# Edge stage of a hybrid conv/attention kernel: the indirect gathers of a chunk gated by the column count of an earlier chunk

## Chip, cores, metric

The kernel runs on one core of one Trainium2 chip. The metric is the device time of one execution in microseconds (us).

## What is computed

The kernel runs a whole network of six layers on 8 images of 32 x 32 x 128 (retention, 3x3 convolution, windowed sum, mixture of 16 experts, windowed attention, and a last mixture of 4 experts whose gates come from a graph attention layer). The change touches only the graph attention. Cut to that:

```
h = (x_flat @ W_gat).reshape(M, 4, 4)                  # M = 8192 nodes, 4 heads of 4
src, dst = edge_index plus one self loop per node      # 524288 edges
e = leaky_relu(a_src[src] + a_dst[dst], 0.2)
ee = exp(e - max over the edges of the same dst)
denom = segment_sum(ee, dst)
agg = segment_sum(h[src] * ee / denom[dst], dst)       # then layernorm, top-2 gates
out = sum over 4 experts of gate * (gelu(x @ W1 + b1) @ W2 + b2)
```

## The kernel before

Edges are sorted and reduced before this stage, so that each of the 128 partitions holds columns of edge keys. A *column* is 128 edges, one a partition; a *chunk* is 16 columns (CHUNK); a *turn* is two chunks (AHEAD = 2), which use buffer halves s = 0 and 1. In the profiled execution TensorE does 320 columns, so 20 chunks, numbered 0 to 19, in ten turns. The first eight turns are a plain loop and the others stand behind a check of the number of edges left.

Each engine has its own program, and they meet by semaphores.

- GpSimd, `fetch(c, s)` (L941 to L948): waits until VectorE has written the indices of chunk c (`records_used`), does a marker instruction (`take_wait`, L813), and then issues 32 indirect DMAs: for each column one gather of 128 source records of 20 floats from `src_dram` and one of 128 target records of 4 floats from `dst_dram` (L947). Each increments `gathered[s]` by 16 when landed. There are 21 fetches, for chunks 0 to 20.
- VectorE, `edge_turn` (L2600 on): for each column t of chunk c the product `rh[:, t % 4]` (L2597, 128 x 1280 floats, from `spread_columns`, L2594 on) of a one-hot matrix and the weighted values, in a ring of RH = 4 buffers. After column 12 (FFN_AT) of chunk c it prepares chunk c+1 (`prepare`, L2565 on: two one-hot matrices) and calls `attend` for it (L2574 on), which waits for all 32 gathers of chunk c+1 to land. Then it does columns 12 to 15, waits for ScalarE's exponential (L1882), weighs the values, and writes the indices of chunk c+3 (`index`, L2558 on, in the half that chunk c+1 has just finished with), which releases GpSimd. So the fetch of a chunk c can begin when VectorE is at the end of chunk c-3, and must have landed by column 12 of chunk c-1.
- TensorE, `edge_column` (L1481 on): waits for the product of a column, adds it into three PSUM banks with three matmuls (six records in the profile), and increments `scattered` (L1489). For the first six turns (chunks 0 to 11) each column is followed by a quarter of an expert step of the last layer (`expert_part`, L1463 on, L1472 and L1478: two records).
- ScalarE, `experts` (L1884 on): the gelu (L1890) and the bias (L1895) of these expert steps, and the exponential of a chunk (L1882). SP stores each expert result in DRAM (L776).

`scattered` is the counter that the change touches. It starts with one increment of RH = 4 from TensorE (L1459) and grows by one for each finished column. VectorE waits for it before each column, so that buffer t % 4 is free:

```
dve.wait_ge(scattered, c * CHUNK + (t + 1))
```

`since(eng, signal, value)` is a wait that leaves itself out where the value is a constant of zero or less. The window stage before the edge stage also has runs of indirect DMAs, 16 gathers of 512-byte rows each (`gather_made`, L917), beside VectorE, ScalarE and TensorE work of the attention layer.

## Time and profile before

| | us |
|---|---|
| median of 3 runs | 4359.78 |
| lowest and highest | 4357.78, 4380.45 |
| profiled execution, device time | 4385.87 |
| its span | 4384.0 |
| TensorE busy (share of the span) | 3178.3 (72%) |
| VectorE busy | 2720.1 (62%) |
| ScalarE busy | 1739.6 (40%) |
| GpSimd busy | 1541.9 (35%) |

PE is TensorE's matmuls, PEld its weight loads, DVE VectorE, ACT ScalarE, POOL GpSimd and SP SyncE. Times are counted from the start of the span. The number in brackets after an instruction of a timeline is the engine's idle time just before it, with what ended it; "remote" there means that the profile names no instruction of this core as the one that ended the wait, and "issue" that it shows nothing that was waited for. A row with a count merges several instructions that follow each other.

### The profile page before, as it was taken

What the parts mean: (1) busy time and instruction counts of PE and PEld (TensorE: products, weight loads), DVE (VectorE), ACT (ScalarE), POOL (GpSimd) and SP (SyncE); (2) the same over time, 40 slices, a digit from 0 to 9 for tenths busy, and PEclk for the clock granted to TensorE, in tenths of its full rate; (3) what the DMA queues carried; (4) which work ended last, traced back from release to release, by engine and by line L of the source; (5) the groups of instructions that cost most, each with busy time, mean ns of one, the idle gap of its engine ahead of it and who ended that gap; (6) DMA issues with size and microseconds to landing.
All of it is one profiled execution on the core that took longest, in us unless ns stands there. A gap on an engine that the chain in (4) does not pass through costs nothing.

```text
span 4384.0 us, 50073 instructions
## 1 busy us (share of the span) xinstructions
PE 3178.3 (72%) x13837; PEld 1510.7 (34%) x13839; DVE 2720.1 (62%) x3836; ACT 1739.6 (40%) x3383; POOL 1541.9 (35%) x1297
## 2 busy tenths in 40 slices
PE   1799999999956637763477888658786787766648
PEld 0222222222212216651355666224343333433322
DVE  2678787787837769997755666215344343554467
ACT  0587787777845625542333454321111111000000
POOL 0211111111003459997333220343443534444500
PEclk9999999999976759996677777679898888877878
DMA  6544234442311127762011010111010100000014
GB/s 214 140 130 121 48 116 120 128 109 55 94 59 62 68 75 239 215 206 82 20 33 29 26 36 12 45 39 27 18 22 22 22 19 18 11 3 3 4 48 182
DMA packets 247387, 319.87 MB, mean 73 GB/s; under 512 B 52301, under 2 KB 183437, under 8 KB 246681
## 3 DMA queue, kind: packets, MB, share of 16 engines
q1 hardware_dynamic: 217496, 296.77, 22.2%
q0 software_dynamic: 29696, 20.97, 2.9%
q8 instruction: 67, 1.10, 0.1%
q14 instruction: 128, 1.04, 0.1%
HBM read 170.95 MB, written 146.67 MB: 72 GB/s over the span
## 4 chain that ended last, share of the span: by engine, by line
PE 23%; another core or an unknown queue 15%; DVE 7%; issue 5%; ACT 1%; DMA 1%; DVEq 0%; SPq 0%; ACTq 0%
PE banks L1487 10%; PE banks L1307 2%; PE banks L1478 2%; PE banks L1472 2%; PE banks L1367 1%; DVE arena L2408 1%; PE banks L1375 1%; PE banks L1350 1%; DVE keys L2363 1%; DMA keys<-experts_dram 1%; PE banks L1551 1%; PE banks L1399 0%; DVE mx L2420 0%; ACT arena L1815 0%
## 5 line engine op out<-in xcount | busy, mean ns | idle before, releaser
L1487 PE MATMUL banks<-arena 128*128 128x512 f32 (+1 forms) x1920 | 804.4, 567 | 192.6 <-DVE arena L2597 126.0
L2597 DVE TENSOR_TENSOR arena<-arena,banks 128x1280 f32<-128x1280 f32 x320 | 466.3, 1485 | 673.0 <-remote 454.6
L1487 PEld LDWEIGHTS banks<-arena 128*128 128x128 f32 x1920 | 393.4, 207 | 663.3 <-issue 511.9
L2127 DVE TENSOR_TENSOR arena<-banks,arena 128x512 f32<-128x512 f32 x512 | 317.7, 683 | 108.6 <-PE banks L1000 82.6
L813 POOL TENSOR_TENSOR pool_spare<-pool_spare 128x1 f32<-128x1 f32 x54 | 16.7, 309 | 1001.3 <-DVE edges_now L2562 703.4
L947 POOL DMA_INDIRECT arena<-src_dram,edges_now x336 | 318.1, 947 | 105.9 <-issue 105.9
L2127 DVE TENSOR_TENSOR keys<-banks,arena 128x512 f32<-128x512 f32 x512 | 317.7, 683 | 60.6 <-PE banks L1000 37.8
L947 POOL DMA_INDIRECT arena<-dst_dram,edges_now x336 | 317.8, 946 | 102.5 <-issue 102.5
L904 POOL TENSOR_TENSOR arena<-arena 128x256 f32<-128x256 f32 x144 | 339.4, 2391 | 17.4 <-ACT arena L1787 17.2
L2363 DVE TENSOR_TENSOR keys<-keys 128x2048 f32<-128x2048 f32 x132 | 339.6, 2612 | 1.9
L1666 ACT ACTIVATE arena<-arena 128x512 f32<-128x512 f32 x512 | 287.0, 619 | 130.6 <-DVE arena L2127 89.1
L1000 PE MATMUL banks<-arena 96*128 96x512 bf16 x1024 | 281.6, 389 | 41.6 <-DVE arena L2127 31.6
L1666 ACT ACTIVATE keys<-keys 128x512 f32<-128x512 f32 x512 | 281.1, 617 | 55.3 <-PE banks L1023 46.7
L1478 PE MATMUL banks<-arena 128*128 128x512 f32 x256 | 154.7, 697 | 183.7 <-ACT arena L1890 177.0
L1895 ACT ACTIVATE keys<-banks,mb 128x512 f32<-128x512 f32 x64 | 44.0, 687 | 528.5 <-remote 304.2
L1844 ACT ACTIVATE arena<-arena,mx 128x128 f32<-128x128 f32 x256 | 99.6, 391 | 332.7 <-DVE mx L2421 318.0
L835 POOL TENSOR_TENSOR work<-work,keys 128x512 f32<-128x512 f32 x32 | 41.0, 1280 | 504.3 <-ACT keys L1602 504.3
L1307 PE MATMUL banks<-arena 128*128 128x64 bf16 x1152 | 151.2, 306 | 86.3 <-DVE arena L2408 74.8
L1000 PEld LDWEIGHTS banks<-arena 96*128 96x128 bf16 x1024 | 80.6, 98 | 346.8 <-DVE arena L2127 122.9
L1890 ACT ACTIVATE arena<-banks,mb 128x512 f32<-128x512 f32 x128 | 86.6, 687 | 266.8 <-remote 112.5
L825 POOL TENSOR_TENSOR keys<-keys 128x512 f32<-128x512 f32 x32 | 40.7, 1271 | 399.9 <-DVE keys L2034 399.9
L1307 PEld LDWEIGHTS banks<-arena 128*128 128x128 bf16 x1152 | 142.7, 148 | 109.6 <-DVE arena L2408 85.1
(399 smaller groups left out, 5804.8 us busy)
## 6 DMA issues: line engine op xcount, KB each, us to landing
sorted_dram<-zeros SPq DMA_DIRECT2D x8, 8192.0 KB, 29.1
arena<-in_w SPq DMA_DIRECT2D x150, 384.0 KB, 4.0
arena<-parts_dram SPq DMA_DIRECT2D x192, 128.0 KB, 4.8
experts_dram<-keys SPq DMA_DIRECT2D x64, 256.0 KB
keys<-experts_dram SPq DMA_DIRECT2D x8, 2048.0 KB, 8.6
parts_dram<-nodes SPq DMA_DIRECT2D x16, 768.0 KB, 3.3
slot_out_dram<-arena SPq DMA_DIRECT2D x40, 256.0 KB, 4.4
arena<-sorted_dram SPq DMA_DIRECT2D x150, 64.0 KB, 3.3
```

Of the source, the lines that this page charges most:

```text
L904: pool.tensor_tensor(slot_hid[:, j % RING], slot_silu[:, j % RING], slot_up[:, j % RING], ALU.mult)\
L947: pool.indirect_dma_start(to[:, s, t, :], None, table[:, :], bass.IndirectOffsetOnAxis(edges_now[:, s, n, t:t + 1].bitcast(U32), 0)).then_ ...
L1000: pe.matmul(banks[:, j, :], k_st[0:STACK, head, a * P:(a + 1) * P], q_st[0:STACK, head, halves(qh)], start=True, stop=True).then_inc(score ...
L1307: last = pe.matmul(out, count_low[:, r, :, t], count_high[:, r, :, t], start=start and t == 0, stop=stop and t == CHUNK - 1, skip_group_ch ...
L1472: pe.matmul(banks[:, 4 + c, :], m1[:, e, c * P:(c + 1) * P], xn_pair[s][:, halves(h)], start=True, stop=True).then_inc(m_h, 1)
L1478: pe.matmul(banks[:, 6 + i % 2, :], m2[:, e, c, :], mh[:, 2 * (i % 2) + c, :], start=(c == 0), stop=(c == CHUNKS - 1)).then_inc(m_out, 1)
L1487: last = pe.matmul(banks[:, bank, 0:part.shape[1]], ohl[:, s, t, :], part, start=False, stop=False, skip_group_check=True)
L1666: act.activation(a_slots[r % 2][:, j, :], p_slots[r % 2][:, j, :], ACT.Abs).then_inc(absolute, 1)
L1844: act.activation(sc[:, k % 2, j, :], sc[:, k % 2, j, :], ACT.Exp, bias=mx[:, k % 2, 1, j:j + 1], accum_out=mx[:, k % 2, 2, j:j + 1]).then_ ...
L2127: dve.tensor_tensor(p_slots[r % 2][:, j, :], banks[:, j, :], table[:, PER_GROUP * g + j, at:at + HALF], ALU.mult).then_inc(masked, 1)
L2363: dve.tensor_tensor(vo[:, t], vi[:, 0], vi[:, 1], ALU.max if t else ALU.min).then_inc(sort_step, 1)
L2597: dve.tensor_tensor(rh[:, t % RH], oha[:, s, t:t + 1, :].broadcast_to([P, VALS, NB]), vals[:, t, :].unsqueeze(2).broadcast_to([P, VALS, NB ...
```

## The change

GpSimd gets, before the gathers of each even column t, a wait for `scattered` and a no-operation that carries it. The value is 16 c + t - 12. So that it is positive for the chunks at the start, `scattered` begins at RH + CHUNK = 20 in place of RH = 4, and VectorE's waits for it are raised by CHUNK = 16. With the start value of 20, a value of 16 c + t - 12 is reached when 16 (c - 2) + t columns are finished by TensorE, that is, t columns of chunk c-2. Four gathers (two columns of sources and targets) stand between two such waits.

```diff
@@ fetch (GpSimd) @@
                 for t in range(CHUNK):
+                    if t % 2 == 0:
+                        since(pool, scattered, c * CHUNK + (RH - CHUNK + t))
+                        pool.nop(nofuse=True)
                     for n, (to, table) in enumerate(((srcrec, src_dram), (dstrec, dst_dram))):
@@ TensorE, the clearing matmuls @@
-            last.then_inc(scattered, RH)
+            last.then_inc(scattered, RH + CHUNK)
@@ spread_columns (VectorE) @@
-                    dve.wait_ge(scattered, c * CHUNK + (t + 1))
+                    dve.wait_ge(scattered, c * CHUNK + (CHUNK + t + 1))
@@ VectorE, before the first prepare @@
-            dve.wait_ge(scattered, RH)
+            dve.wait_ge(scattered, RH + CHUNK)
```

## Rows read from the trace of the kernel before

**Rows 1.** The page: busy tenths of POOL in 40 equal slices of the span.

```profile
POOL 0211111111003459997333220343443534444500
```

**Rows 2.** Waits, 2911 to 4203 us: who for whom, total us, times, longest.

```profile
POOL pool_spare L813 <- DVE edges_now L2562: 501.8, 19, 32.9
DVE arena L2597 <- remote: 454.6, 48, 18.9
...
ACT keys L1895 <- remote: 286.0, 12, 28.8
```

**Rows 3.** Timeline of GpSimd, one fetch: start us, duration us, instruction.

```profile
3262.24 0.96 POOL L947 DMA_INDIRECT arena<-src_dram,edges_now  x1 [0.49 <-issue]
...
3301.02 0.94 POOL L947 DMA_INDIRECT arena<-dst_dram,edges_now  x1 [0.30 <-issue]
```

**Rows 4.** Timeline of TensorE in the same chunk.

```profile
3260.66 2.31 PE L1487 MATMUL banks<-arena 128*128 128x512 f32 x6
...
3284.72 2.31 PE L1487 MATMUL banks<-arena 128*128 128x512 f32 x6
3286.86 1.02 PE L1472 MATMUL banks<-work,arena 128*128 128x512 f32 x2
...
3308.69 2.08 PE L1478 MATMUL banks<-arena 128*128 128x512 f32 x2 [13.74 <-ACT arena L1890]
```

**Rows 5.** Timelines of VectorE and ScalarE in the same chunk.

```profile
3276.47 1.49 DVE L2597 TENSOR_TENSOR arena<-arena,banks 128x1280 f32<-128x1280 f32 x1 [2.94 <-PE banks L1487]
3289.83 1.49 DVE L2597 TENSOR_TENSOR arena<-arena,banks 128x1280 f32<-128x1280 f32 x1 [11.88 <-remote]
3306.65 5.68 DVE L2597 TENSOR_TENSOR arena<-arena,banks 128x1280 f32<-128x1280 f32 x4 [15.34 <-remote]
...
3307.37 0.69 ACT L1895 ACTIVATE keys<-banks,mb 128x512 f32<-128x512 f32 x1 [27.39 <-remote]
```

**Rows 6.** Timelines of TensorE and ScalarE, the last two chunks.

```profile
4162.31 45.07 PE L1487 MATMUL banks<-arena 128*128 128x512 f32 x120 [2.48 <-DVE arena L2597]
...
4160.89 0.26 ACT L1882 ACTIVATE arena<-arena 128x64 f32<-128x64 f32 x1 [59.63 <-DVE arena L2582]
4197.10 0.26 ACT L1882 ACTIVATE arena<-arena 128x64 f32<-128x64 f32 x1 [35.95 <-DVE arena L2582]
```

**Rows 7.** Timeline of GpSimd: the markers of the fetches in chunks 0, 12, 18.

```profile
2911.39 0.19 POOL L813 TENSOR_TENSOR pool_spare<-pool_spare 128x1 f32<-128x1 f32 x1 [32.48 <-DVE edges_now L2562]
...
3744.35 0.20 POOL L813 TENSOR_TENSOR pool_spare<-pool_spare 128x1 f32<-128x1 f32 x1 [28.05 <-DVE edges_now L2562]
...
4108.10 0.19 POOL L813 TENSOR_TENSOR pool_spare<-pool_spare 128x1 f32<-128x1 f32 x1 [19.46 <-DVE edges_now L2562]
```

**Rows 8.** Timelines of GpSimd and VectorE: a run of 16 gathers.

```profile
2191.32 1.19 POOL L917 DMA_INDIRECT arena<-slot_out_dram,arena  x1 [0.18 <-issue]
...
2210.65 0.94 POOL L917 DMA_INDIRECT arena<-slot_out_dram,arena  x1 [0.30 <-issue]
...
2214.17 1.89 DVE L2456 SCALAR_TENSOR_TENSOR work<-banks,bout,work 128x512 f32<-128x512 f32 x3 [14.37 <-remote]
```

**Rows 9.** Timeline and waits (2560 to 2592 us): a looser run of 16.

```profile
2560.45 1.02 POOL L917 DMA_INDIRECT arena<-slot_out_dram,arena  x1 [0.45 <-issue]
2566.14 0.95 POOL L917 DMA_INDIRECT arena<-slot_out_dram,arena  x1 [4.67 <-issue]
...
2585.84 1.34 POOL L917 DMA_INDIRECT arena<-slot_out_dram,arena  x1 [0.30 <-issue]
...
DVE work L2456 <- PE banks L1394: 4.3, 1, 4.3
```

**Rows 10.** Timelines of GpSimd and ScalarE: the end of 64 gathers in one run.

```profile
2877.96 0.95 POOL L947 DMA_INDIRECT arena<-dst_dram,edges_now  x1 [0.30 <-issue]
...
2886.09 0.69 ACT L1890 ACTIVATE arena<-banks,mb 128x512 f32<-128x512 f32 x1 [4.21 <-remote]
```

**Rows 11.** Windows: busy us of each engine, TensorE's granted clock, DMA share, GB/s.

```profile
2911.00:3745.00 834.00, 640.32 (x1536) 309.16 (x1537) 352.19 (x363) 135.53 (x188) 365.90 (x397) 0.87 0.10 22
```

## Prediction

> **What bounds the kernel now.** The page's slices come first [rows 1]: POOL's tenths show the gathers that the change edits, from slice 26 on (some 2800 us), with POOL never over half busy. That stretch is the edge stage. The waits of 2911 to 4203 us come next [rows 2]. Three numbers matter. VectorE's column product (L2597) waits 454.6 us in 48 pieces for something the profile can't name ("remote"), ScalarE's L1895 waits 286.0 us in the same way, and GpSimd waits 501.8 us for the next chunk's indices, so it is idle a good third of the stage.
>
> The timeline of one chunk tells what the nameless waits are. GpSimd issues the chunk's 32 gathers from 3262.24 to 3301.96, (3301.02 - 3262.24) / 31 = 1.25 us apart [rows 3]. TensorE keeps a pace of (3284.72 - 3260.66) / 8 = 3.01 us a column (six matmul records of 2.31 us in all, and an expert part of two) until 3287.9, and then stands 13.74 us before the next expert part [rows 4]. VectorE's products at 3289.83 and 3306.65 come 11.88 and 15.34 us after the last, and ScalarE's L1895 comes after 27.39 us of idling [rows 5]. VectorE froze at 3276.47 + 1.49 = 3277.96, 15.7 us into the gathers, when 12 or 13 were out. ScalarE and VectorE both run freely again at 3306.65 to 3307.37, some 5.4 us after the last gather ended. So a dense run of gathers freezes two engines that have nothing to do with it, and TensorE starves.
>
> One chunk is the control. Chunk 19 has no gathers beside it: TensorE does 20 columns in 45.07 us without a gap, 2.25 us each, and ScalarE's exponentials are 35.95 us apart, where the chunk before took 59.63 [rows 6]. A chunk's gathers thus cost 24 us there. With the experts beside it, 12 chunks (0 to 11) take (3744.35 - 2911.39) / 12 = 69.4 us [rows 7], against 16 x 3.01 = 48.2 us of unbroken TensorE: 21.2 us of freezing each. Chunks 12 to 17 take (4108.10 - 3744.35) / 6 = 60.6 us [rows 7].
>
> **Why spacing can help.** The freeze must depend on density for the change to be worth anything. The window stage has runs of 16 gathers. The run from 2191.32 to 2210.65 is 1.29 us apart and froze VectorE for 14.4 us, until 2214.17, 2.6 us after its last gather [rows 8]. The run from 2560.45 to 2585.84 is 1.69 us apart (one pause of 4.67 us after its first gather), and the longest wait of VectorE's L2456 in it is 4.3 us, for a named TensorE matmul, with no nameless wait in the whole view [rows 9]. The thaw comes 2.6 us after 16 gathers and 5.4 us after 32, so each gather leaves (5.4 - 2.6) / 16 = 0.18 us of undone work: something serves a gather in 1.25 + 0.18 = 1.43 us. After 64 in one run ScalarE's last late operation starts at 2886.09, 7.2 us after the end at 2878.91, which says less per gather, (7.2 - 5.4) / 32 = 0.06 [rows 10]. My service time is 1.43 us, an estimate, the upper of the two, as it comes from runs of the length at issue.
>
> **The change part by part.** *The counter* starts at 20 in place of 4 and VectorE waits for 16 more: the same wait on the same column, one immediate, cost nothing.
>
> *The gate.* Per chunk GpSimd gets 8 waits with a no-operation to carry each, 7 with effect inside a chunk and the first at its border. The gate of columns t and t+1 opens when TensorE (it is TensorE's count, so a column that is multiplied) has finished t columns of the chunk two places ahead. Its own price does not show in the trace; the bounds are nothing (it fits in the 0.30 us between two gathers) and the 0.49 us between GpSimd's marker and its first gather [rows 3], so 0 to 4 us a chunk. I take 0.15 each, 1.2 us a chunk, nearer to the plain gap because only one instruction and a register sum are added. While GpSimd waits anyway it is hidden; in the chunks without experts it is not, but there it spaces.
>
> *What queues behind it.* Behind a closed gate stand the rest of the chunk's gathers and the next chunk's fetch, and only VectorE's attend waits for them, at its twelfth column of the next chunk. The last gate opens at 14 of 16 columns, so the last four gathers end about 6 us into the next chunk. VectorE, up to four columns ahead of TensorE, asks for them 8 x 3.01 = 24 us into it, so some 18 us are spare. SP's queue is not passed; its expert stores share the DMA engines with the gathers and meet them thinner.
>
> *Chunks with experts (0 to 11).* Two columns take 6.02 us and four gathers 5.0 us, so the gate holds and gathers come every 6.02 / 4 = 1.50 us, over 1.43: no backlog and no freeze, 48.2 us a chunk. The margin is 5%, so I put 49.5 us. 12 x (69.4 - 49.5) = 239 us saved. Who is late next is TensorE alone: VectorE's 16 products of 1.49 us [rows 5] and its preparation fit in 48 us.
>
> *Chunks without experts (12 to 18).* Two columns take 4.5 us, less than four gathers, so the gate is open whenever TensorE is at pace and does not space anything. The run freezes VectorE after about 16 us as before, TensorE uses up its four columns (9 us) and stops, the gate shuts, GpSimd pauses, and the backlog of some 3 us drains. Such a cycle is 16 + 9 + 3 = 28 us for about 20 gathers, 1.4 us each, or 45 us a chunk; TensorE restarts at half clock (2.08 us for the two-matmul part that takes 1.02 [rows 4]), which adds about 5. I take 50 us: 7 x (60.6 - 50) = 74 us saved. The bounds are GpSimd's own 32 x 1.25 + 3 = 43 us and today's 60.6.
>
> *Sum.* 239 + 74 = 313 us. The profiled execution took 4385.87 us (span 4384.0), so it would take 4073. The median of the three runs is 4359.78, 26.1 lower; against it the forecast is 4359.8 - 313 = 4047 us.
>
> **The rivals.**
> 1. *Only the chunks with experts gain* (the change does not do what it says in the rest, where the gate never shuts). For it: the 4.5 against 5.0 us. Against it: a frozen TensorE does shut the gate. 4359.8 - 239 = 4121 us. Chance 0.15.
> 2. *The freeze comes later but comes.* If a gather's service is nearer 1.69 than 1.43, the margin of 5% is none, and only half of the freezing goes: 4359.8 - 313 / 2 = 4203 us. For it: no row of the trace lies between 1.29 and 1.69. Chance 0.13.
> 3. *The freezes are not the gathers'* but belong to fetching the loop's code or to something periodic; then 4360 us. Against it: the last chunk runs the same code without one [rows 6]. Chance 0.04. The Trainium skill speaks for this one twice. "Runtime: NRT & Kernel Launch", section "Instruction fetch mechanics", says that a taken branch out of the loaded window stalls until the page is fetched; by that rule the stalls would stay, and the trace disagrees in the last chunk. "Trainium Architecture — The Big Picture", section "What this means for kernel authors", says that SBUF's engine side and DMA side can't contend and that only the port pair of VectorE and GpSimd is a lock; by that rule gathers could not hold up ScalarE and the sum would be 0 us, and ScalarE's 27.39 us disagree [rows 5].
> 4. *Slower: rest is what resets the freeze, not density.* Today the first 12 gathers of a chunk are free after 20 to 30 us of idle GpSimd. If a pause under 1 us gives back none of that, all 32 pay. A paying gather costs 21.2 / 20 = 1.06 us with experts and 24 / 20 = 1.2 without, so 12 x 12 x 1.06 + 7 x 12 x 1.2 = 253 us more: 4613 us. It decides from the second chunk on, where the rest has gone. Against it: the looser run of 16 went by with no nameless wait [rows 9], although it also had fewer than 32. Chance 0.06.
>
> **How the numbers follow.** The forecast has 0.62, and its own range is 3975 (48.2 and 43 us a chunk: 12 x 21.2 + 7 x 17.6 = 378 us saved, 3982, less a few us) to 4100. The full range reaches up through rivals 1 and 2, to 4205, and leaves out rivals 3 and 4 and the tails, about 0.15. Half a per cent, 22 us, is about what a measurement of this kernel can tell from no change. Faster by more: 0.62 + 0.15 + 0.13 = 0.90. Within: 0.04. Slower by more: 0.06.
>
> **What would show it.** In the changed profile, gathers of chunks 2 to 13 come in fours every 6.0 us with a pause of about a microsecond; the nameless waits of L2597 and L1895 are near 0 before chunk 12; GpSimd's markers are 48 to 50 us apart there and 43 to 52 us after; TensorE's granted clock in that stretch rises from 0.87 [rows 11] to near 1. The forecast is wrong if nameless waits of over 5 us go on inside the expert chunks (rival 2), if chunks 12 to 18 stay at 60 us (rival 1), or if freezes fill whole chunks (rival 4).

## The result, and the profile after

The changed kernel takes 4012.34 us (median of 4 runs, 4007.11 to 4034.18) where the kernel before, on the same chip, takes 4370.11 us (4 runs, 4357.78 to 4386.33). The ratio is 0.9189, 95% interval 0.9138 to 0.9239. The forecast was 4047 us, in a range of 3975 to 4205, so the direction and the range hold and the gain was somewhat larger than the sum.

The profiled execution took 4014.97 us, with a span of 4013.1 us, 370.9 us less than the one before. First the page of the changed kernel: engine totals, the slices of GpSimd and of TensorE's granted clock, and the groups of the edge stage (busy, mean ns | idle before, and what ended it). Line numbers are three higher than before: L950 is the gather, L2600 the column product, L1490 its matmuls, L1893 the experts' gelu and L1898 their bias.

```profile
PE 3101.9 (77%) x13837; PEld 1493.8 (37%) x13839; DVE 2725.1 (68%) x3836; ACT 1743.6 (43%) x3383; POOL 1545.4 (39%) x1297
POOL 0211111111110256799873222202466666666500
PEclk9999999999996675899856777677799999999968
L1490 PE MATMUL banks<-arena 128*128 128x512 f32 (+1 forms) x1920 | 742.9, 533 | 57.5 <-DVE arena L2600 53.0
L2600 DVE TENSOR_TENSOR arena<-arena,banks 128x1280 f32<-128x1280 f32 x320 | 468.8, 1486 | 318.2 <-PE banks L1490 222.4
L950 POOL DMA_INDIRECT arena<-src_dram,edges_now x336 | 318.4, 948 | 241.0 <-PE banks L1490 115.7
```

GpSimd's tenths in the edge stage now stand at 6 in eight slices running, where they changed between 3 and 5 [rows 1]. The gathers are as long and as many as before; what changed is that their engine waits for TensorE (the last line), and VectorE's wait is for TensorE too.

The waits of the changed kernel, from 2900 to 3830 us (sum, times, longest), answer to [rows 2]:

```profile
DVE arena L2600 <- PE banks L1490: 222.4, 146, 8.5
DVE arena L2600 <- remote: 44.7, 11, 8.3
POOL arena L950 <- PE banks L1490: 116.9, 69, 12.3
POOL arena L950 <- remote: 30.9, 8, 4.7
ACT arena L1893 <- remote: 4.3, 2, 2.2
```

VectorE's nameless waits fell from 454.6 to 44.7 us. ScalarE's were 286.0 us in the bias [rows 2] and 90.0 in the gelu (L1890, in the same view); now the bias has none and the gelu (L1893) 4.3. Nearly all of what is left lies in the chunks without experts: 43.8 of VectorE's 44.7 us are from 3481 to 3835, and all 30.9 of GpSimd's. These last are new. GpSimd too now has waits that the profile can't name.

GpSimd in an expert chunk (start, busy, line, [idle before]) comes in fours, as [rows 3] did not:

```profile
3454.77 0.94 POOL L950 DMA_INDIRECT arena<-src_dram,edges_now  x1 [1.32 <-PE banks L1490]
3456.01 0.95 POOL L950 DMA_INDIRECT arena<-dst_dram,edges_now  x1 [0.30 <-issue]
...
3458.51 0.95 POOL L950 DMA_INDIRECT arena<-dst_dram,edges_now  x1 [0.30 <-issue]
3460.78 0.95 POOL L950 DMA_INDIRECT arena<-src_dram,edges_now  x1 [1.32 <-PE banks L1490]
```

From one four to the next are 3460.78 - 3454.77 = 6.01 us, 1.50 a gather.

ScalarE's exponentials mark the chunks best, as there is one at the same point of each. Those of chunks 0, 12 and 20 (the last is the one past chunk 19) in the kernel before, and then in the changed one:

```profile
2909.82 0.26 ACT L1882 ACTIVATE arena<-arena 128x64 f32<-128x64 f32 x1
3742.67 0.26 ACT L1882 ACTIVATE arena<-arena 128x64 f32<-128x64 f32 x1
...
4197.10 0.26 ACT L1882 ACTIVATE arena<-arena 128x64 f32<-128x64 f32 x1 [35.95 <-DVE arena L2582]
```

```profile
2888.20 0.26 ACT L1885 ACTIVATE arena<-arena 128x64 f32<-128x64 f32 x1
3468.91 0.26 ACT L1885 ACTIVATE arena<-arena 128x64 f32<-128x64 f32 x1
...
3825.04 0.26 ACT L1885 ACTIVATE arena<-arena 128x64 f32<-128x64 f32 x1 [37.02 <-DVE arena L2585]
```

The stretch with experts (12 chunks, called A below) went from 832.9 to 580.7 us, 69.4 to 48.4 a chunk, and saves 252. The stretch behind it (B, eight intervals, the last without gathers beside it) went from 454.4 to 356.1 and saves 98. Together 350 of the 370.9 us. Of the rest, 21.6 lie ahead of chunk 0's exponential (2909.82 against 2888.20) and do not belong to the change: GpSimd's marker that opens the stage stood between 2764 and 2802 us in thirteen of the fourteen kernels traced here (2753 in the other), and what comes ahead of it is work that no edit touches.

The windows of the changed kernel over the two stretches (length, then PE, PEld, DVE, ACT and POOL busy, the granted clock, DMA share, GB/s), to be held against [rows 11]:

```profile
2889.80:3481.00 591.20, 590.38 (x1563) 297.37 (x1564) 362.45 (x364) 140.32 (x190) 367.86 (x399) 1.00 0.14 31
3481.00:3850.00 369.00, 296.78 (x763) 149.93 (x761) 228.44 (x236) 2.06 (x8) 211.86 (x229) 0.92 0.08 4
```

With experts TensorE is busy for 590.38 of 591.20 us, and granted 1.00 (its higher level, 2.4 GHz) where it had 0.87. That stretch has next to nothing left but TensorE's own work.

### The profile page after: what moved, and what is told of

It is laid out like the page before. It is cut to its first block and busy times, and to the rows that moved or that the text cites. A ratio compares the mean times of both kernels' runs of the same rounds, so it can differ in the third digit from the quotient of the medians.

```text
span 4013.1 us, 50374 instructions
## 1 busy us (share of the span) xinstructions
PE 3101.9 (77%) x13837; PEld 1493.8 (37%) x13839; DVE 2725.1 (68%) x3836; ACT 1743.6 (43%) x3383; POOL 1545.4 (39%) x1297
## 5 line engine op out<-in xcount | busy, mean ns | idle before, releaser
L1490 PE MATMUL banks<-arena 128*128 128x512 f32 (+1 forms) x1920 | 742.9, 533 | 57.5 <-DVE arena L2600 53.0
L2600 DVE TENSOR_TENSOR arena<-arena,banks 128x1280 f32<-128x1280 f32 x320 | 468.8, 1486 | 318.2 <-PE banks L1490 222.4
L1490 PEld LDWEIGHTS banks<-arena 128*128 128x128 f32 x1920 | 370.3, 194 | 481.0 <-issue 414.1
L950 POOL DMA_INDIRECT arena<-src_dram,edges_now x336 | 318.4, 948 | 241.0 <-PE banks L1490 115.7
L950 POOL DMA_INDIRECT arena<-dst_dram,edges_now x336 | 318.0, 947 | 109.9 <-issue 108.7
L2130 DVE TENSOR_TENSOR keys<-banks,arena 128x512 f32<-128x512 f32 x512 | 317.8, 684 | 60.8 <-PE banks L1003 38.3
L1003 PE MATMUL banks<-arena 96*128 96x512 bf16 x1024 | 282.6, 390 | 40.4 <-DVE arena L2130 30.9
L1893 ACT ACTIVATE arena<-banks,mb 128x512 f32<-128x512 f32 x128 | 87.9, 688 | 237.2 <-PE banks L1475 128.0
L1481 PE MATMUL banks<-arena 128*128 128x512 f32 x256 | 138.4, 631 | 53.1 <-ACT arena L1893 40.5
L917 POOL DMA_INDIRECT arena<-slot_out_dram,arena x128 | 159.8, 1249 | 43.1 <-issue 42.9
```

The lines of the kernel that those rows point to most:

```text
L917: pool.indirect_dma_start(made[:, j, :], None, slot_out_dram[:, :], bass.IndirectOffsetOnAxis(rows_now[:, j:j + 1].bitcast(U32), 0)).then_ ...
L950: pool.indirect_dma_start(to[:, s, t, :], None, table[:, :], bass.IndirectOffsetOnAxis(edges_now[:, s, n, t:t + 1].bitcast(U32), 0)).then_ ...
L1003: pe.matmul(banks[:, j, :], k_st[0:STACK, head, a * P:(a + 1) * P], q_st[0:STACK, head, halves(qh)], start=True, stop=True).then_inc(score ...
L1481: pe.matmul(banks[:, 6 + i % 2, :], m2[:, e, c, :], mh[:, 2 * (i % 2) + c, :], start=(c == 0), stop=(c == CHUNKS - 1)).then_inc(m_out, 1)
L1490: last = pe.matmul(banks[:, bank, 0:part.shape[1]], ohl[:, s, t, :], part, start=False, stop=False, skip_group_check=True)
L2130: dve.tensor_tensor(p_slots[r % 2][:, j, :], banks[:, j, :], table[:, PER_GROUP * g + j, at:at + HALF], ALU.mult).then_inc(masked, 1)
```

## The experiments

Each kernel is either the kernel before or the changed one with the edit shown. "Lead" is the time from GpSimd's first marker of the stage to chunk 0's exponential, A and B are the stretches above. "Thaw" is the time from the first gather of a run to the start of the operation that ends the last long nameless wait in it (ScalarE's, in the chunks with experts). The table gathers the results (a dash: not read), and each kernel is taken up below. Times are those of the profiled executions for the two kernels of the case, else medians or single runs; lead, A and B are read in each kernel's one profiled execution. The kernels ran on different chips, and the kernel before had medians of 4354 to 4378 us beside them.

| kernel | us | lead | A (a chunk) | B |
|---|---|---|---|---|
| before (profiled execution) | 4385.87 | 111.5 | 832.9 (69.4) | 454.4 |
| changed (profiled execution) | 4014.97 | 110.8 | 580.7 (48.4) | 356.1 |
| instruction between, no wait | 4313.97 | - | 822.2 (68.5) | 445.1 |
| gate for expert chunks alone | 4107.62 | 113.0 | 579.0 (48.3) | 450.8 |
| gate every 8 columns | 4118.99 | 110.7 | 652.1 (54.3) | 390.6 |
| gate every column | 4019.22 | 115.9 | 579.0 (48.3) | 351.5 |
| paced to 1.335 us, no gate | 4260.82 | 99.6 | 764.0 (63.7) | 417.3 |
| paced to 1.389 us | 4126.09 | 94.1 | 682.1 (56.8) | 379.9 |
| paced to 1.446 us | 3958.68 | 49.9 | 580.7 (48.4) | 354.2 |
| paced by a longer fill | 4014.41 | 52.6 | 602.7 (50.2) | 400.3 |
| small source records | 4352.70 | - | 827.0 (68.9) | 450.5 |
| half of the records | 4379.28 | - | 842.5 (70.2) | 458.1 |
| changed, once more | 4012.55 | 110.7 | 580.6 (48.4) | 352.6 |
| gate, and a paced lead | 3989.10 | 49.7 | 607.9 (50.7) | 356.8 |

### Is it the wait, or any instruction between the gathers?

On the kernel before:

```diff
                 for t in range(CHUNK):
+                    if t % 2 == 0:
+                        pool.nop(nofuse=True)
```

> The kernel before with the eight no-operations of a fetch and no wait in front of them. Backlog theory (each gather leaves 0.18 us undone at a distance of 1.25 us, and the freeze starts when some 2 us have piled up): the gathers stay at 1.25 to 1.3 us, chunks with experts stay at 68 to 70 us and the others at 60 to 61, time within 1% of before, 4330 to 4400 us. Rival (any break in the stream of gathers, even an instruction between them, is enough): near the changed kernel, 4010 to 4100 us.

Measured 4313.97 us in one run (4378.02 before on the same chip). The 64 us look like a gain, but the edge stage began some 46 us earlier, while A and B together are only 20 us shorter, and each chunk still freezes at the same point: the thaw comes 44.9 to 45.1 us after the first gather (44.6 in the first fetch behind the lead). The no-operation alone does next to nothing. It is the wait that counts.

### Which chunks does the gate help?

On the changed kernel, the gate is left off in the fetches of chunks 14 on:

```diff
-            def fetch(c, s):
+            def fetch(c, s, gated=True):
...
-                    if t % 2 == 0:
+                    if gated and t % 2 == 0:
...
-            with pool.Fori(0, IMAGES) as turn:
+            with pool.Fori(0, IMAGES - LEAD) as turn:
...
+            for turn in range(IMAGES - LEAD, IMAGES):
+                fetch(turn * AHEAD + 1, 1, turn == IMAGES - LEAD)
+                fetch(turn * AHEAD + 2, 0, False)
...
-                            fetch(turn * AHEAD + 1, 1)
-                            fetch(turn * AHEAD + 2, 0)
+                            fetch(turn * AHEAD + 1, 1, False)
+                            fetch(turn * AHEAD + 2, 0, False)
```

> The changed kernel with the gate only in the fetches of chunks 1 to 13, that is, beside the chunks with experts; the fetches of chunks 14 to 20 are ungated. If the gate works in both stretches as the changed profile reads (252 us from chunks 0 to 11, 98 us from 12 to 19), this takes the changed time plus 98 us, about 4110 us, with ungated chunks of 60 us. Rival (the chunks without experts gained only because the stage came into them with less backlog): under 4040 us.

4107.62 us: A stays at 579.0 and B goes back to 450.8, that of the kernel before. So in B too it is the wait in front of the gathers that saves the 98 us, although a column there (2.25 us) is quicker than its two gathers. The timeline of the changed kernel shows how. GpSimd, in the fetch of chunk 15:

```profile
3525.78 0.96 POOL L950 DMA_INDIRECT arena<-src_dram,edges_now  x1 [2.62 <-PE banks L1490]
...
3549.59 0.95 POOL L950 DMA_INDIRECT arena<-dst_dram,edges_now  x1 [0.30 <-issue]
3554.81 0.95 POOL L950 DMA_INDIRECT arena<-src_dram,edges_now  x1 [4.27 <-remote]
```

VectorE beside it:

```profile
3552.61 5.74 DVE L2600 TENSOR_TENSOR arena<-arena,banks 128x1280 f32<-128x1280 f32 x4 [6.64 <-remote]
```

And TensorE:

```profile
3519.46 28.09 PE L1490 MATMUL banks<-arena 128*128 128x512 f32 x78
3554.15 24.70 PE L1490 MATMUL banks<-arena 128*128 128x512 f32 x60 [6.61 <-DVE arena L2600]
```

Twenty gathers run without a pause from 3525.78 on. VectorE then stands 6.64 us before its product at 3552.61, TensorE runs dry and stands 6.61 us, and GpSimd stands 4.27 us before the 21st gather. The cycle is 3554.81 - 3525.78 = 29.03 us for 20 gathers, 1.45 each. GpSimd's markers in this stretch are (3756.31 - 3522.95) / 5 = 46.7 us apart.

It looks as if a dry TensorE had shut the gate, but it had not. The trace has all 1920 matmul records of the 320 columns, six each, so the columns can be counted. This gate asks for ten columns of chunk 13. The 78 records in the first row above are the last column of chunk 12 and twelve of chunk 13, and the tenth of these was finished at 3543.25, 7.3 us before GpSimd came to the gate at 3550.54. The same count for all eleven pauses of over 1 us that GpSimd makes at a gate from the fetch of chunk 15 on finds the columns finished 1.2 to 9.0 us before it came (and likewise finished before it came for 14 and 11 pauses in two kernels below, the changed one once more and the one with a gate every column). In this stretch GpSimd is not held back by an unfinished column. It is caught by the freeze itself, in the wait that the change gave it, and so ends its dense run after some 20 gathers in place of 32. What is late is taken up below. Whether a wait for a column long finished would do as well was not tried.

### How dense may the gathers be in a burst?

On the changed kernel, one gate for eight columns, and in another kernel one for every column:

```diff
-                    if t % 2 == 0:
+                    if t % 8 == 0:
```

> The changed kernel with a gate at every eighth column in place of every second: the same mean rate beside the experts, but in runs of 16 gathers. Backlog theory: it peaks at 16 x 0.18 = 2.9 us, so nameless waits of 3 to 8 us show in ScalarE and VectorE at the end of each run, partly hidden by the four columns in hand; chunks with experts 48 to 54 us, time 4010 to 4100 us. Rival (only the mean rate counts): no nameless waits, 48.1 us a chunk, equal to the changed kernel within 0.5%.

4118.99 us and 54.3 us a chunk in A, a little over the upper end of what was expected. Runs of 16 gathers freeze a little each time. GpSimd's first and last gather of one such run:

```profile
3058.62 0.95 POOL L950 DMA_INDIRECT arena<-src_dram,edges_now  x1 [9.64 <-PE banks L1490]
...
3077.35 0.94 POOL L950 DMA_INDIRECT arena<-dst_dram,edges_now  x1 [0.30 <-issue]
```

and ScalarE at its end:

```profile
3081.21 0.69 ACT L1893 ACTIVATE arena<-banks,mb 128x512 f32<-128x512 f32 x1 [1.51 <-remote]
```

The last nameless wait ends 3081.21 - 3058.62 = 22.59 us after the first gather, 1.41 us for each of 16, although GpSimd had put the last of them behind it at 3078.29. In the kernel before, 32 gathers from 3262.24 thaw at 3307.37 [rows 3, 5]: 45.13 us, 1.41 for each again. That was the first sign that the thaw counts from the first gather and not from the last.

> The changed kernel with a gate before every column, two gathers each, in place of four for every two columns. Service theory: beside the experts the rate is the same 1.50 us and nothing was frozen, so no change there; in the chunks without experts GpSimd pays 16 gates in place of 8, at under 0.1 us each. Within 0.5% of the changed kernel, 3990 to 4040 us. Rival (each gate costs GpSimd 0.3 us or more): 20 us or more slower than the changed kernel.

The gate at every column took 4019.22 us, within 0.2% of 4012.34. Twice as many gates cost nothing that can be seen. Nor does an open gate in a dense run: in the 20 gathers above every step across an open gate is the plain 1.25 us (from the first gather to the last of the 20, 3549.59 - 3525.78 = 23.81 us, over 19).

### The gathers paced by GpSimd itself, without a gate

If only the spacing counts, a small fill behind each gather should do as well. On the kernel before, with N columns to fill (128, 192, 256, 384):

```diff
                             edges_now[:, s, n, t:t + 1].bitcast(U32), 0)).then_inc(gathered[s], 16)
+                        since(pool, made_summed, c * (2 * CHUNK) + (2 * IMAGES + 2 * t + n))
+                        pool.nop(nofuse=True)
+                        pool.memset(arena[:, 21632:21632 + N], 0.0).then_inc(made_summed, 1)
```

The wait in front of a fill is for the fill before it, of the same engine. With N = 128:

> The kernel before, ungated, with a no-operation and a memset of 128 x 128 floats after every gather, so that GpSimd paces itself, at an expected 1.45 to 1.6 us a gather, with no pause over 0.7 us. Backlog theory: no freezes at all, chunks with experts 48 to 49 us, the others 32 x the distance = 47 to 51 us, and the stretch before chunk 0, with 64 gathers in one run, falls from 111 to 60 to 105 us (it can't be shorter than 32 gathers and the expert steps); time 3960 to 4060 us. Rival (a pause of about a microsecond or waits on TensorE's count are what helps): freezes stay, 4250 us or more.

A miss: 4260.82 us. The fill was shorter than I had assumed and the gathers came 1.335 us apart, not 1.45 or more, so this is not a test of the value aimed at. It is a good one of the law, though. GpSimd's first and last gather of a chunk, and the ScalarE operation that ends its last nameless wait:

```profile
3398.27 0.96 POOL L947 DMA_INDIRECT arena<-src_dram,edges_now  x1 [0.48 <-issue]
...
3439.67 0.95 POOL L947 DMA_INDIRECT arena<-dst_dram,edges_now  x1 [0.17 <-POOL arena L951]
```

```profile
3443.71 1.26 ACT L1893 ACTIVATE arena<-banks,mb 128x512 f32<-128x512 f32 x2 [4.97 <-remote]
```

The thaw is 45.44 us behind the first gather, as before, but only 3443.71 - 3440.62 = 3.1 us behind the last. With N = 256:

> The kernel before, ungated, with a no-operation and a memset of 128 x 256 floats after every gather: an expected 1.44 us from gather to gather, 0.1 more than with the memset of 128 x 128. The runs so far have the thaw 45.1 to 45.4 us after the first of 32 gathers, at 1.25 and at 1.335 us apart alike, and 22.6 us after the first of 16, so a gather is served in 1.41 us. Service theory: at 1.44 us nothing piles up and no freeze is left anywhere; chunks with experts 48.1 us, the others 46 to 47.5 us, 60 to 70 us from the first marker to the first exponential in place of 111, in all 3940 to 3985 us, faster than the changed kernel. Rival (a steady run needs pauses, as the gates give): freezes go on, 4200 us or more.

3958.68 us (4 runs, 3954.05 to 3965.34), ratio 0.9081, interval 0.9038 to 0.9124, as expected and clearly below the changed kernel's. Two gathers in a row in it (with the fill between them), and the windows of lead, A and B:

```profile
3249.72 0.33 POOL L951 MEMSET arena<- 128x256 f32 x1
3250.21 0.95 POOL L947 DMA_INDIRECT arena<-dst_dram,edges_now  x1 [0.17 <-POOL arena L951]
...
3251.66 0.95 POOL L947 DMA_INDIRECT arena<-src_dram,edges_now  x1 [0.16 <-issue]
```

```profile
2792.00:2842.00 50.00, 49.58 (x107) 18.89 (x105) 5.33 (x12) 28.06 (x40) 43.78 (x71) 0.98 0.28 81
2842.00:3423.00 581.00, 578.55 (x1531) 291.38 (x1532) 357.77 (x360) 137.08 (x188) 509.32 (x807) 1.00 0.14 32
3423.00:3777.00 354.00, 290.57 (x770) 150.82 (x768) 231.72 (x237) 6.46 (x13) 308.52 (x489) 0.91 0.09 5
```

The gathers come 1.44 us apart (1.446 with the step at each chunk's border), in the lead and from chunk to chunk, with one step of 3.0 to 3.3 us in each 96 of them, and VectorE's waits for its product, from 2842 to 3777 us, show what is left of 454.6 us of nameless ones:

```profile
DVE arena L2600 <- remote: 5.6, 2, 2.8
```

ScalarE has two more, of 1.5 and 3.6 us. The lead, which the gate does not reach, falls from 111 us to 49.9. The windows of the changed kernel's lead show what was there:

```profile
2777.00:2889.80 112.80, 60.48 (x107) 21.89 (x105) 6.77 (x19) 29.48 (x43) 61.03 (x67) 0.74 0.15 39
```

The same 107 matmul records lie in 112.8 us there and in 50.0 here. The two kernels' medians differ by 4012.55 - 3958.68 = 53.9 us, on two chips (the kernel before had 4367.66 beside the one and 4354.03 beside the other), and the leads by 110.7 - 49.9 = 60.8, while A and B agree within 2 us: the lead accounts for the difference. In B the paced kernel is bound by GpSimd (markers 46.3 us apart), which leaves it no better than the gate.

With N = 384, to see that more spacing costs (a buffer of its own for this fill did not fit in SBUF, with 1536 bytes needed and 256 free, so it too goes to the arena, which all these fills use):

> The kernel before, ungated, with a no-operation and a memset of 128 x 384 floats after every gather, an expected 1.55 us from gather to gather. Service theory (1.41 us a gather, measured by the thaw 45 us after the first of 32 at any pace): no freezes; 32 x 1.55 + 0.3 = 49.9 us a fetch is over TensorE's 48.1, so GpSimd bounds every chunk at 50 us: 1.6 x 12 us and 3.4 x 7 us more than at the 1.446 us pace, about 4000 us. Rival (the freezes at the 1.446 us pace were still partly there): no slower than that pace.

4014.41 us: GpSimd needs 49.7 us a chunk and sets the pace throughout, A 50.2 a chunk and B 400.3. It has no nameless wait of a microsecond in the whole stage. With N = 192, to come nearer to the limit from above:

> The same with a memset of 128 x 192 floats, an expected 1.39 us a gather, just under the service time. Service theory: 0.02 us a gather piles up, under 0.7 us in a chunk, which the 3 us of idle GpSimd beside the experts clear; beside the chunks without experts there is no idle time and after two to four chunks a freeze comes. Chunks with experts 48.1 us, the others 45.5 to 50 us, 3940 to 3985 us in all, within 0.5% of the 1.446 us pace. Rival (the limit lies above 1.41, only the 1.446 us pace passes): freezes in every chunk, over 4050 us.

4126.09 us (4 runs, 4112.66 to 4136.57; ratio 0.9432, interval 0.9384 to 0.9479), against the expectation. The gathers are 1.389 us apart, and every chunk with experts freezes, in most from 14 to 23 us into its gathers on (in one after 37); those without experts freeze less regularly. The first and last gather, and ScalarE's thaw:

```profile
3233.15 0.96 POOL L947 DMA_INDIRECT arena<-src_dram,edges_now  x1 [0.48 <-issue]
...
3276.20 0.95 POOL L947 DMA_INDIRECT arena<-dst_dram,edges_now  x1 [0.16 <-issue]
```

```profile
3279.10 0.69 ACT L1898 ACTIVATE keys<-banks,mb 128x512 f32<-128x512 f32 x1 [12.21 <-remote]
```

3279.10 - 3233.15 = 45.95 us. At 1.389 the gathers are 0.02 us too quick each, at 1.44 they are slow enough but for small waits, and at 1.55 without any. The limit of 45.1 / 32 = 1.41 fits that; no run lies nearer to it.

### What is it that takes 1.41 us?

Bytes or records would be the first guess. On the kernel before, first both gathers of a column from the table of targets, four floats a record (this changes which values the source records hold), then both as before but for partitions 0 to 63 alone (the records of partitions 64 to 127 are left out):

```diff
-for n, (to, table) in enumerate(((srcrec, src_dram), (dstrec, dst_dram))):
-    pool.indirect_dma_start(to[:, s, t, :], None, table[:, :], ...
+for n, (to, table) in enumerate(((srcrec, dst_dram), (dstrec, dst_dram))):
+    pool.indirect_dma_start(to[:, s, t, 0:GH], None, table[:, :], ...
```

```diff
-    pool.indirect_dma_start(to[:, s, t, :], None, ...
-        edges_now[:, s, n, t:t + 1].bitcast(U32), 0)).then_inc(gathered[s], 16)
+    pool.indirect_dma_start(to[0:P // 2, s, t, :], None, ...
+        edges_now[0:P // 2, s, n, t:t + 1].bitcast(U32), 0)).then_inc(gathered[s], 16)
```

> The kernel before with the source gathers fetching 4 floats a record from the target table in place of 20 from the source table, so the attention is computed from other values and the rest of each record is left as it was; the count of gathers and of records is the same, the bytes are a third. If a gather's 1.41 us are for the number of records or for the DMA as such, nothing changes: thaw 45 us after the first gather, 4310 to 4400 us. If they are for bytes, the freezes go: 4000 to 4060 us.

> The kernel before with every gather of the edge stage for partitions 0 to 63 alone; the other 64 partitions of the records are left out. 64 records a gather in place of 128. If the 1.41 us are for the records, a gather is served in 0.7 to 0.9 us, and unless GpSimd also issues faster than that there is no freeze and the time is 3950 to 4060 us. If they are for the gather as such, the thaw stays 45 us after the first gather or comes relative to the end as before, and the time stays over 4250 us.

4352.7 and 4379.28 us, with 4354.03 for the kernel before on that chip: nothing gained by either. The smaller records leave spacing (1.25) and thaw where they were. Half the records shorten GpSimd's own part, 0.90 us in place of 0.95 and 1.205 from one gather to the next, but not the thaw. GpSimd's first and last gather of a chunk, and ScalarE behind it:

```profile
3179.48 0.90 POOL L947 DMA_INDIRECT arena<-src_dram,edges_now  x1 [0.48 <-issue]
...
3216.83 0.90 POOL L947 DMA_INDIRECT arena<-dst_dram,edges_now  x1 [0.31 <-issue]
```

```profile
3224.45 0.69 ACT L1895 ACTIVATE keys<-banks,mb 128x512 f32<-128x512 f32 x1 [15.61 <-remote]
```

44.97 us behind the first gather and 3224.45 - 3217.73 = 6.7 behind the last. GpSimd is quicker, so the backlog is longer, and the freeze begins sooner (9.0 us in at the earliest, where it was 11.3 with 1.25 us, both without the first fetch behind the lead, where VectorE froze after 4.9 in either kernel). Together, in the chunks with experts and in runs without a pause:

| gathers in a run | apart | thaw after the first | a gather |
|---|---|---|---|
| 16 (gate every 8 columns) | 1.25 | 22.4 to 22.7 | 1.40 to 1.42 |
| 32 (kernel before) | 1.25 | 45.1 to 45.4 | 1.41 to 1.42 |
| 32 (half of the records) | 1.205 | 44.9 to 45.1 | 1.40 to 1.41 |
| 32 (small records) | 1.25 | 44.9 to 45.1 | 1.40 to 1.41 |
| 32 (paced) | 1.335 | 45.3 to 45.4 | 1.42 |
| 32 (paced) | 1.389 | 45.3 to 46.1 | 1.42 to 1.44 |

It is not the data that take so long. In the kernel before, the last of the 1024 DMA packets of the run from 3262.24 starts 40.8 us after the first gather, 1.1 us behind the last gather's record, and from 3303.2 to the thaw (3307.3) the core's DMA queues move nothing at all:

```profile
DMA packets 0, 0.00 MB, mean 0 GB/s; under 512 B 0, under 2 KB 0, under 8 KB 0
```

**What is late are TensorE's signals.** ScalarE's bias at 3307.37 [rows 5] waits for this matmul, which by its record had ended at 3281.87, 25.5 us before (the end is modelled, but TensorE had started its next work at 3281.71 and kept its pace of 3.01 us a column [rows 4]):

```profile
3280.85 1.02 PE L1478 MATMUL banks<-arena 128*128 128x512 f32 x2
```

Besides the instructions, the trace has the time of most semaphore updates, that is, of the signals by which engines release each other. In that chunk TensorE ends a column every 3.01 us, at 3271.99, 3275.00, 3278.01 and so on, but the updates of `scattered` are at 3276.44, 3289.80, 3306.63, 3307.42, 3307.54 and 3307.66, and VectorE's products start 0.02 to 0.03 us behind the first three of these [rows 5]. Over the whole edge stage of the kernel before, 174 of TensorE's 479 recorded updates come more than 0.3 us after the end of the last instruction that can have made them, up to 25.5 us. Of the 675 that VectorE and ScalarE made, none comes over 0.02 us late. At 1.55 us a gather none of TensorE's 510 is late, and at 1.44 there are 48 of 434, by 2.2 us at most.

And in all fourteen traces every nameless wait of over 0.5 us of VectorE and ScalarE in the edge stage, and of GpSimd at its gates, ends with an update of one of three semaphores that TensorE alone raises. (Four waits of GpSimd for its own fill, 1.2 us at most, are the only others.) So neither VectorE nor ScalarE is slowed: VectorE's product takes 1.47 to 1.49 us in every kernel. They wait for word of work that TensorE's records show as done. GpSimd had no wait for TensorE before. The gate gave it one, and that is why it stands still in the freezes of B.

### What is left of it: the lead

> The changed kernel again, beside the self-paced one on the same chip. 4000 to 4035 us; the self-paced kernels stay 40 to 60 us below it.

The changed kernel again, on the chip of the kernels paced to 1.389 us and by the longer fill: 4012.55 us (4 runs), ratio 0.9195, interval 0.9146 to 0.9244. Then the gate kept, with the fetches of chunks 0 and 1 paced by the fill of 256 columns and not gated:

```diff
-                    if t % 2 == 0:
+                    if t % 2 == 0 and not paced:
...
+                        if paced:
+                            pool.wait_ge(made_summed, c * (2 * CHUNK) + (2 * IMAGES + 2 * t + n))
+                            pool.nop(nofuse=True)
+                            pool.memset(arena[:, 21632:21888], 0.0).then_inc(made_summed, 1)
-            fetch(0, 0)
-            with pool.Fori(0, IMAGES) as turn:
+            fetch(0, 0, True)
+            fetch(1, 1, True)
+            fetch(2, 0)
+            with pool.Fori(1, IMAGES) as turn:
```

> The changed kernel, with the fetches of chunks 0 and 1 ungated and self-paced at 1.446 us by a no-operation and a memset of 128 x 256 floats after each gather; all later fetches gated as in the change. Service theory: the expert steps ahead of chunk 0 are no longer frozen, and the first marker to the first exponential takes 50 us in place of 111. But GpSimd then comes into the stage some 40 us behind TensorE, so the gates of the fetch of chunk 2 are open and don't space it: it runs at 1.25 us and freezes, until TensorE has lost the lead again, 20 to 35 us in the first two or three chunks. After that 48.1 and 46.4 us a chunk. 3970 to 3995 us, under the changed kernel and over the self-paced one. Rival (the gates space the gathers wherever they stand): 3945 to 3965 us, equal to the self-paced one.

3989.1 us (4 runs, 3972.47 to 4002.26; ratio 0.9118, interval 0.908 to 0.9155). The lead is 49.7 us, as in the wholly paced kernel, but the first chunk now takes 77.2 us (in the changed kernel 51.5). The lead ends sooner, so TensorE starts on chunk 0 while GpSimd is still behind. From the fetch of chunk 2 on GpSimd finds its gates open and issues 20 gathers 1.25 us apart, and VectorE and ScalarE freeze for over 13 us, until GpSimd too is caught at a gate. (Smaller nameless waits, of up to 5.8 us, came before that, beside gathers still paced at 1.44 us. Why here and not in the wholly paced kernel is open.) So nearly half of the 61 us is lost again (A 607.9 in place of 580.6). A gate that hangs on the consumer spaces only a GpSimd that is ahead. The fill spaces it in either case, and that kernel, at 3958.68 us, has the lowest median, although its interval and this one's overlap.

## Why the prediction was right, and where it was off

**The mechanism, and the saving with experts: right, and short by 13 us.** Dense gathers cause the freezes and spacing ends them, as written down. What is held up are TensorE's signals and not, as the prediction took it, VectorE and ScalarE themselves; for this part of the sum that makes no difference. The step "48.2 us a chunk" plus a margin gave 49.5 and 239 us; 48.4 and 252 were measured. The margin was the error. It was put in because 1.50 is only 5% over 1.43, and the runs show that the limit is sharp: at 1.44 us the paced kernel has only small nameless waits left, at 1.389 it freezes in every such chunk. The 0.87 to 1.00 of the clock came as forecast, and so did the fours every 6.0 us.

**The saving without experts: near in size, short by 24 us, and wrong in its main step.** The cycle that was written down is freeze, TensorE dry, gate shut, drain, 28 us for about 20 gathers, and 29.0 us for 20 were measured. But the gate was not shut. Its columns were finished 1.2 to 9.0 us before GpSimd came, and what held GpSimd was the late signal, which the prediction did not know of. The parts don't fit either: VectorE froze 20.2 us into the run and not 16, and TensorE stood 1.6 us later and not 9. That the sum came so close was luck. The same step stands as the argument against rival 1 ("a frozen TensorE does shut the gate"), so the rival was turned down for a reason that does not hold. The 5 us a chunk put on top for TensorE's restart at half clock was mis-sized: the markers are 46.7 us apart, not 50. TensorE has 36 us of work in a chunk that GpSimd holds at over 45, so the slow restart fits in its slack. The 98 us saved against 74 are this term.

**The gate's price: 0.15 us each was too much.** It was taken inside 0 to 0.49. The steps across open gates are the plain 1.25 outside a freeze, and twice as many gates make no difference. The value is at the lower bound, nothing that can be seen.

**The service time: 1.43 us estimated, 1.41 measured.** It came from two thaws behind the last gather. Counted from the first gather, as the experiments showed that it has to be, one run of 32 gives it at once. The 64 of the lead give (2886.09 - 2799.04) / 64 = 1.36 (their first gather begins at 2799.04), a little off the others, as in the prediction; those of the changed kernel, which the gate does not reach, give 89.94 / 64 = 1.41.

**The threshold of twelve gathers: wrong, without cost to the forecast.** The prediction took it that a freeze needs some 16 us or about 2 us of backlog. At 1.25 us ScalarE's or VectorE's first long nameless wait already began 11.3 us in, in most chunks, and 6.8 in the second runs of 16. At 1.389 it began 14 to 23 us in, when at 0.02 us each the backlog was 0.2 to 0.4 us. The onset moves with the density (9 us at 1.205, 11.3 at 1.25, 11.3 to 16 at 1.335), but by no fixed backlog. What sets it is open.

**A reading.** The 35.95 and 59.63 us of rows 6 are ScalarE's idle times before the exponentials. The exponentials are 36.2 and 59.9 us apart, and the difference of 24 us is the same.

**The rivals.** That only the expert chunks gain (4121 us) is ruled out for this kernel, and the kernel with the gate in those chunks alone shows what it would have been: 4107.62 us, close to that price. That the freeze comes anyway, at a service near 1.69, is ruled out by 1.41. That the freezes are not the gathers' is ruled out by the paced kernel, which has the same loop and 5.6 us of VectorE's nameless waits. "Trainium Architecture — The Big Picture", section "What this means for kernel authors", of the Trainium skill says that SBUF's engine side and its DMA side can't contend. The prediction took ScalarE's 27.39 us as disagreeing with it. They don't: the engines' own instructions are as long beside the gathers as without them, and what comes late are TensorE's signals. The rule is not tested by this case, and the 350 us saved say nothing against it. That rest and not density is needed (4613 us) is ruled out by the kernels at 1.44 and 1.55 us: all gathers of the stage with no step over 3.3 us between two of them, and no nameless wait of over 3.6 us in the one and of 1 us in the other.

**The sum against the median.** The edge stage saved 350 us where the sum had 313. The profiled executions differ by 370.9 us, the medians by 357.8, as the stage's start moves by some 20 us from run to run for reasons that were not studied.

## What to carry to other kernels

Signals between two engines can come late because of a third engine's DMAs, to which neither has any tie. It shows as nameless waits on two engines at once that end a fixed time after a dense run's first DMA. Before you blame the engines that stand, count what they wait for: here the work was long done. The cure is the spacing, found by trying some and not by thinning the data. Space by something that holds whether the issuing engine is ahead or behind. A gate on the consumer costs nothing that can be seen, but it is open just when a late engine catches up. A filler works in either case, and the size matters by hundredths of a microsecond on the short side (1.389 against 1.44), while too long costs less. Look at the stretch ahead of the loop too; here a start of 64 ungated gathers was worth 54 us, over half of what the chunks without experts gave.

## What the runs showed of the hardware that was not expected

- A dense run of indirect DMAs from GpSimd makes TensorE's semaphore updates late, by up to 25.5 us, while those of VectorE and ScalarE keep to 0.02 us. It lasts until N x 1.41 us after the first of N, whatever they carry: 128 records or 64, source records cut to four floats or whole. GpSimd issues one every 1.25 us (1.205 with 64 records), and their data move at that pace.
- The updates are not stopped outright. Those of the chunk above come at 3272.87, 3276.44, 3279.26, 3289.80, 3295.43, 3306.63 and 3307.34, distances of about 5, 4, 15, 8, 16 and 1 times 0.70 us, half of 1.41. TensorE goes on as long as it has data. "Perfetto Trace Analysis", section "Per-instruction lifecycle: what the profiler-reported window actually captures", of the Trainium skill says that the record of a DMA issued by GpSimd ends when the descriptors are written and not when the data have moved. The trace agrees: the record of the gather at 3262.24 ends at 3263.20, and its data are reported as landed from 3264.29 to 3264.54.
- The limit is sharp: 1.389 us apart gives 4126 us, 1.446 (with the borders) gives 3959, and 1.335 gives 4261.
- Still open are where TensorE's updates are held up, why TensorE's alone (GpSimd's own were late 13 times, by 2.5 us at most, in the kernels at 1.335 and 1.389), and what sets the onset. The gathers' own updates, sixteen each, are a candidate. Taking them away would test it, but it leaves their readers with nothing to wait for, and it was not tried.
